# One row tile for the second FFN bias, one product for the shifts, strips of 32 columns, and new step lists

## The chip, the cores and the metric

One core of one Trainium2 chip runs the whole kernel; seven others are idle. The metric is the device time of one execution in microseconds (us), the median of three runs. Five engines work side by side, each through its own list of instructions: TensorE (PE in the profile; its weight loads are shown as PEld), VectorE (DVE), ScalarE (ACT), GpSimd (POOL) and SyncE (SP), which issues the transfers. Semaphores order them.

## What is computed

`x` is 16 images of 16 x 16 positions with 96 channels, so 4096 tokens. Cut to what matters, the reference is:

```python
x = x + leaky_relu(top-2 of 5 experts, mixed(groupnorm(x) @ We + be))     # "conv"
t = tokens(x)                                                             # [16, 256, 96]
n = layernorm(t)
k, q, v = n @ wk, n @ wq, n @ wv                                          # 6 heads of 16
wei = softmax(causal(k @ q.T / 96**0.5))                                  # 256 x 256 a head
t = t + (wei @ v) @ wproj + bproj
n = layernorm(t)
h = gelu(n @ w1[e] + b1[e])                                               # 4 experts, 384 hidden
y = h @ w2[e] + b2[e]                                                     # b2: the second FFN bias
t = t + sum over e of weight[e] * y[e]                                    # top 2 of 4
```

All inputs and outputs are float32.

## The kernel before, in words

The 16 images are worked on in eight units of two images, so 512 tokens (four tiles of 128) a unit. A step is named `kind.index@unit`, and `ORDER` holds one list of steps for each engine, written out by a planner; the order of the work is that of these lists, and semaphores hold each step until its data is there. A step of TensorE carries the PSUM bank it writes after a colon. `warm.6@0:1` are six products that compute nothing used and fill a wait.

The steps that matter here:

- `conv`, `norm1_t`, `qk`, `score`, `prob`, `gate2`: whole products or transposes of up to 128 columns.
- `v` (L872), `proj` (L961) and the products of `ffn2` (L1010): float32 products with the tokens as the stationary side, in strips of `STRIP` = 64 tokens, which write 64 partitions of PSUM each and can run two side by side. A float32 product is two instructions in the trace. `pv` (L946) has always been 32 columns wide, four side by side.
- `ffn1.m` (L988, L989): the first FFN layer of one block of 128 hidden columns, two products of 512 tokens. The rest of its contraction, 32 of the rows, is done for three blocks at once by `rest1.e` (L994): three products of 32 rows each at partitions 0, 32 and 64. It is a step of its own in the list. ScalarE's GELU (L793) of a block waits for it.
- `ffn2.e` (L996 to L1014): the second layer of expert `e`. First the bias, a product of 128 rows (`ones_b` times `b2_parts`, L1003), whose three parts of b2 stand at rows 0, 32 and 64 with zeros between them; GpSimd puts them there (L616 to L622). Then 24 float32 products in strips, which are 48 instructions. VectorE adds the result to the residual (L1266).
- `shift`: VectorE splits the negated row maxima of the scores into three bfloat16 parts (L1182 to L1195), TensorE turns them, one transposition of 18 columns for each of four tiles (L912 to L915), ScalarE copies the [18, 512] result (L758), and SyncE places it in `k_stack` (L513), where the products of `prob` need it.

Of the kernel before, what the change touches and what calls it, by code (L numbers as in the profile page):

```python
# [30 lines left out]
STRIP = 64  # L31
# [35 lines left out]
        prob.0.1@1:5 prob.0.2@1:0 prob.0.3@1:6 prob.0.4@1:4 prob.1.0@1:1 prob.1.1@1:5 proj@0:3 prob.1.2@1:0
        prob.1.3@1:6 conv.3@5:4 prob.1.4@1:2 warm.3@12:1 score.0.0@2:1 score.0.1@2:5 score.0.2@2:0 score.0.3@2:3
        score.0.4@2:6 score.1.0@2:2 score.1.1@2:4 norm2_t@0:1 score.1.2@2:5 pv.0@1:0 score.1.3@2:3 norm1_t@3:6
        score.1.4@2:2 pv.1@1:1 qk.0@3:4 qk.1@3:5 gate2@0:6 ffn1.0@0:0 ffn1.1@0:4 ffn1.2@0:5 rest1.0@0:-1 ffn1.3@0:3  # L70
        ffn1.4@0:2 proj@1:1 ffn1.5@0:0 rest1.1@0:-1 ffn1.6@0:4 ffn1.7@0:5 ffn1.8@0:3 rest1.2@0:-1 shift@2:2 ffn2.0@0:0
# [1225 lines left out]
```

## Time and profile before

| | |
|---|---|
| median of three runs | 316.29 us (316.01 to 317.96) |
| the profiled execution | 316.23 us, of which the span of the core is 314.5 |
| granted TensorE clock over the span | 0.998 |
| TensorE, VectorE, ScalarE, GpSimd busy | 94%, 76%, 70%, 34% of the span |

The span runs from the first to the last instruction of the core. Times inside it are counted from its start. TensorE's instructions are pipelined and their ends are modelled, so the busy time of TensorE counts overlapping instructions once, and the time from one start to the next is the better measure of what a product costs.

### The profile page before, as it was taken

To read this page: it belongs to the slowest core of one execution; us is meant where nothing else is said; L and a number is where in the kernel's file an instruction comes from. 1 tells how busy PE (TensorE), PEld (TensorE's weight loads), DVE (VectorE), ACT (ScalarE), POOL (GpSimd) and SP (SyncE) were. 2 spreads that over 40 slices of the span, in tenths; PEclk is the share of its full clock that TensorE was granted. 3 is DMA by queue.
4 is the path that set the end of the run, shared out by engine and by line. 5 is a ranking of instruction groups with operands and counts; after the bars stand their busy time and mean duration, and the time that the engine had idled before them with its cause. 6 is when DMAs were issued, how large, how long until landed. Compare 5 with 4: busy or idle time off the path is not lost.

```text
span 314.5 us, 9387 instructions
## 1 busy us (share of the span) xinstructions
PE 297.0 (94%) x3459; PEld 214.7 (68%) x3459; DVE 238.7 (76%) x1050; ACT 221.1 (70%) x441; POOL 106.3 (34%) x176
## 2 busy tenths in 40 slices
PE   5889899998999999999999999999999999999995
PEld 2655445665656877778677786777686787877774
DVE  4769989997899898898899788799738845813433
ACT  2879778886678997787766495773986769472660
POOL 4444567549821450065070006720622041100000
PEclk9999999999999999999999999999999999999999
DMA  7930054625637010034133003610380111002000
GB/s 178 185 41 0 1 120 72 113 83 125 101 82 115 4 45 0 4 96 113 36 81 95 4 3 77 128 31 14 87 112 3 29 27 44 0 10 62 2 27 25
DMA packets 28436, 18.70 MB, mean 59 GB/s; under 512 B 16820, under 2 KB 26952, under 8 KB 28392
## 3 DMA queue, kind: packets, MB, share of 16 engines
q1 hardware_dynamic: 28392, 18.12, 27.4%
q8 instruction: 27, 0.44, 0.7%
q14 instruction: 17, 0.14, 0.2%
HBM read 3.12 MB, written 1.57 MB: 15 GB/s over the span
## 4 chain that ended last, share of the span: by engine, by line
PE 65%; SPq 2%; DMA 1%; ACT 1%; DVE 1%; issue 1%; POOL 1%; DVEq 0%; POOLq 0%; ACTq 0%
PE PS L1010 21%; PE PS L988 8%; PE PS L989 7%; PE PS L994 4%; PE PS L946 4%; PE PS L961 3%; PE PS L862 3%; PE PS L904 2%; PE PS L928 2%; PE PS L1003 2%; PE PS L854 2%; SPq L509 2%; PE PS L893 1%; DMA k_stack<-qk_parts 1%; PE PS L932 1%; PE PS L975 1%
## 5 line engine op out<-in xcount | busy, mean ns | idle before, releaser
L793 ACT ACTIVATE hidden<-PS,b_t 128x512 f32<-128x512 f32 x96 | 59.5, 683 | 33.1 <-PE PS L994 32.9
L1010 PE MATMUL PS<-w_f,hidden 128*64 128x96 f32 x1536 | 70.4, 248 | 0.0
L1010 PEld LDWEIGHTS PS<-w_f,hidden 128*64 128x64 f32 x1536 | 64.4, 137 | 7.0 <-issue 7.0
L1266 DVE SCALAR_TENSOR_TENSOR res<-PS,weight,res 128x96 f32<-128x96 f32 x128 | 31.4, 309 | 35.5 <-PE PS L1010 35.2
L988 PE MATMUL PS<-t_a,w_a 128*128 128x512 f32 x96 | 42.0, 437 | 0.0
L989 PE MATMUL PS<-t_b,w_b 128*128 128x512 f32 x96 | 37.9, 395 | 0.0
L1170 DVE CUSTOM_DVE_ANT_0 masked<-PS,causal 128x128 bf16<-128x128 f32 (+1 forms) x120 | 34.9, 352 | 3.6 <-PE PS L893 2.1
L769 ACT ACTIVATE prob_a<-PS 128x512 f32<-128x512 f32 x48 | 25.9, 601 | 10.8 <-PE PS L928 10.7
L654 POOL TENSOR_SCALAR_AFFINE_SELECT prob_a<-prob_a 128x768 f32<-128x768 f32 x16 | 13.8, 865 | 57.0 <-ACT prob_a L769 57.0
L1131 DVE SCALAR_TENSOR_TENSOR PS<-conv_y,weight,PS 128x96 f32<-128x96 f32 x128 | 30.2, 316 | 2.5 <-ACT PS L721 2.4
L575 POOL TENSOR_TENSOR ln_var<-ln_mv,eps_t 128x4 f32<-128x4 f32 x16 | 3.2, 198 | 74.6 <-DVE ln_mv L1063 74.6
L666 ACT ACTIVATE normed<-res,ln_bias,ln_scale 128x96 f32<-128x96 f32 x64 | 24.6, 458 | 2.7 <-POOL ln_bias L585 2.7
L988 PEld LDWEIGHTS PS<-t_a,w_a 128*128 128x128 f32 x96 | 18.1, 188 | 7.0 <-issue 1.6
L814 PE MATMUL PS<-ones_b 128*128 128x512 bf16 x89 | 22.7, 397 | 0.0
L989 PEld LDWEIGHTS PS<-t_b,w_b 128*128 128x128 f32 x96 | 18.1, 189 | 2.2
L648 POOL TENSOR_TENSOR qk_parts<-qk_rest,qk_parts 96x512 bf16<-96x512 f32 x16 | 18.5, 1158 | 2.4
L711 ACT ACTIVATE conv_y<-PS 128x486 f32<-128x486 f32 x32 | 17.1, 566 | 1.9 <-PE PS L803 1.5
L1181 DVE TENSOR_REDUCE row_max<-PS 128x2 f32<-128x512 f32 (+2 forms) x30 | 16.9, 626 | 0.5 <-PE PS L893 0.5
L862 PE MATMUL PS<-t,qk_w 96*96 96x512 f32 x32 | 15.9, 610 | 1.1 <-ACT t L736 1.0
L904 PE MATMUL PS<-q_stack,k_stack 96*128 96x256 bf16 x96 | 16.8, 273 | 0.0
L582 POOL TENSOR_TENSOR ln_scale<-ln_var,power_t 128x4 f32<-128x4 f32 x16 | 16.2, 1012 | 0.0
L769 ACT ACTIVATE prob_b<-PS 128x512 f32<-128x512 f32 (+1 forms) x32 | 14.7, 499 | 2.0 <-PE PS L932 2.0
(157 smaller groups left out, 613.4 us busy)
## 6 DMA issues: line engine op xcount, KB each, us to landing
q_stack<-qk_parts SPq DMA_DIRECT2D x48, 96.0 KB, 3.2
k_stack<-qk_parts SPq DMA_DIRECT2D x48, 96.0 KB, 3.7
t_c<-t_a SPq DMA_DIRECT2D x24, 64.0 KB, 2.0
out_dram<-res SPq DMA_DIRECT2D x8, 192.0 KB, 2.5
X<-in_x_dram SPq DMA_DIRECT2D x4, 192.0 KB, 2.9
X<-in_x_dram SPq DMA_DIRECT2D x2, 384.0 KB, 5.1
...
```

Of the source, the lines that this page charges most:

```text
L666: act.activation(normed[:, which, t, :], rows[:, t, :], ACT.Identity, bias=ln_bias[:, which, t:t + 1], scale=ln_scale[:, which, t:t + 1]). ...
L769: act.activation(dst, PS[:, bank("prob", n, index), 0:dst.shape[1]], ACT.Exp, scale=SCALE).then_inc(act_emptied["prob"], 1)
L793: act.activation(hidden[:, m, 0:T * P], PS[:, bank("ffn1", n, index), 0:T * P], ACT.Gelu, bias=b1_t[:, m:m + 1]).then_inc(act_emptied["ffn ...
L814: pe.matmul(PS[:, bank("warm", n, index), :], ones_b[:, :], ones_b[:, :].unsqueeze(1).to_broadcast([P, 4, P]), start=True, stop=True)
L862: pe.matmul(PS[0:C, bank("qk", n, index), 0:T * P], qk_w[:, tensor, :], t1s[n % 2][:, 0:T * P], start=True, stop=True).then_inc(filled["qk ...
L904: mm = pe.matmul(dst[:, j * TOKENS:(j + 1) * TOKENS], kk[0:STACK, h, t0 + P:t0 + TOKENS], q[0:STACK, h, t0:t0 + TOKENS], start=n >= MASK_FROM,
L988: pe.matmul(dst, w1_a[:, w], t2_as[n % T2][:, 0:T * P], start=True, stop=False)
L989: pe.matmul(dst, w1_b[:, w], t2_bs[n % T2][:, 0:T * P], start=False, stop=False)
L1010: mm = pe.matmul(PS[strip:strip + STRIP, y, t * C:(t + 1) * C], hidden[:, m, t * P + strip:t * P + strip + STRIP], w2_f[:, m, :], start=Fa ...
L1131: ins = dve.scalar_tensor_tensor(mixed[:, t, :], y, weight0[:, t, e:e + 1], mixed[:, t, :], ALU.mult, ALU.add)
L1170: ins = dve.tensor_tensor_reduce(masked[:, place % 2, j * size:(j + 1) * size], ps[:, j * size:(j + 1) * size], causal[:, TOKENS - size:TO ...
L1266: ins = dve.scalar_tensor_tensor(res2[:, t, :], PS[:, y, t * C:(t + 1) * C], weight1[:, t, e:e + 1], res2[:, t, :], ALU.mult, ALU.add).the ...
```

## The change

- `STRIP` goes from 64 to 32, so `v`, `proj` and `ffn2` have twice as many products, each half as wide.
- The three parts of b2 go to rows 96, 97 and 98 of `b2_parts`. GpSimd splits b2 on one partition, and three transfers of SyncE (`w_b2`) place the parts. The bias product has three rows instead of 128. The zero fills of `b2_f` and `b2_parts` on VectorE go, and b2 is loaded once instead of three times.
- `rest1.e` of the experts 1 to 3 goes into `ffn2.(e-1)`, ahead of its bias; `rest1.0` stays a step. The wait for the expert's GELU moves behind the bias.
- The shift parts lie as [part, head, tile], so one transposition of 72 columns turns them, ScalarE copies [72, 128], and the transfer places 72 rows of 128.
- All five lists are new. TensorE's has 429 steps instead of 459, with 68 warm-up products instead of 89 (counted in the lists).

The lists are cut here to some of their lines.

```diff
@@ -28,7 +28,7 @@
-STRIP = 64
+STRIP = 32
@@ -54,129 +54,125 @@
     PE: """
-        xt@0:0 warm.6@0:1 gavg.0@0:1 xt@1:2 xt@2:3 gavg.1@0 xt@3:4 warm.4@1:5 xt@4:5 xt@5:6 gavg.0@1:0 warm.2@2:2
-        xt@6:2 xt@7:1 gavg.1@1 conv.0@0:3 conv.1@0:4 conv.2@0:5 conv.3@0:6 warm.14@3:2 conv.0@1:2 conv.1@1:0 conv.2@1:1
-        conv.3@1:3 warm.9@4:4 conv.0@2:4 conv.1@2:5 conv.2@2:6 conv.3@2:2 warm.16@5:0 norm1_t@0:0 conv.0@3:1 conv.1@3:3
-        gavg.0@2:4 warm.2@6:5 qk.0@0:5 qk.1@0:6 warm.13@7:2 norm1_t@1:2 conv.2@3:1 conv.3@3:0 warm.3@8:3 gavg.1@2
-        warm.10@9:3 qk.0@1:3 qk.1@1:5 score.0.0@0:6 score.0.1@0:1 score.0.2@0:0 score.0.3@0:4 v@0:2 v@1:3 score.0.4@0:6
-        score.1.0@0:5 score.1.1@0:1 norm1_t@2:0 score.1.2@0:4 score.1.3@0:2 score.1.4@0:3 conv.0@4:6 conv.1@4:5
-        conv.2@4:1 conv.3@4:4 qk.0@2:2 warm.2@10:6 shift@0:6 qk.1@2:3 warm.5@11:0 score.0.0@1:0 score.0.1@1:5
...
-        rest1.1@7:-1 ffn2.3@6:2 ffn1.7@7:6 ffn1.8@7:1 ffn2.0@7:0 ffn1.9@7:3 ffn1.10@7:2 ffn1.11@7:4 rest1.2@7:-1
-        rest1.3@7:-1 ffn2.1@7:0 ffn2.2@7:5 ffn2.3@7:6
+        xt@0:0 warm.6@0:1 gavg.0@0:1 xt@1:2 xt@2:3 gavg.1@0 xt@3:4 warm.9@1:5 gavg.0@1:5 xt@4:6 xt@5:0 xt@6:2 xt@7:1
+        gavg.1@1 conv.0@0:3 conv.1@0:4 conv.2@0:6 conv.3@0:0 warm.13@2:2 gavg.0@2:2 conv.0@1:1 conv.1@1:5 conv.2@1:3
+        conv.3@1:4 conv.0@2:6 conv.1@2:0 gavg.1@2 conv.2@2:1 conv.3@2:5 conv.0@3:3 conv.1@3:4 conv.2@3:2 conv.3@3:6
+        norm1_t@0:0 qk.0@0:1 qk.1@0:5 v@0:0 warm.22@3:3 norm1_t@1:3 qk.0@1:4 warm.6@4:2 score.0.0@0:2 qk.1@1:6
+        score.0.1@0:1 score.0.2@0:5 score.0.3@0:0 score.0.4@0:3 score.1.0@0:4 conv.0@4:2 score.1.1@0:1 score.1.2@0:5
+        score.1.3@0:0 score.1.4@0:6 conv.1@4:3 conv.2@4:4 norm1_t@2:1 conv.3@4:5 warm.9@5:0 qk.0@2:0 shift@0:6 qk.1@2:2
+        score.0.0@1:3 score.0.1@1:1 score.0.2@1:4 score.0.3@1:5 score.0.4@1:6 score.1.0@1:3 score.1.1@1:1 warm.3@6:4
...
+        ffn1.2@7:5 ffn1.3@7:4 ffn1.4@7:3 ffn1.5@7:0 rest1.0@7:-1 ffn2.3@6:1 ffn2.0@7:2 ffn1.6@7:6 ffn1.7@7:5 ffn1.8@7:1
+        ffn1.9@7:4 ffn1.10@7:3 ffn1.11@7:0 ffn2.1@7:2 ffn2.2@7:6 ffn2.3@7:5
...
     SCALAR: """
-        norm1@0 conv.3@2 conv.0@3 leaky@1 norm1_t@0 tanh@2 conv.1@3 qk.0@0 qk.1@0 mix@2 norm1@1 w_w1@0 conv.2@3
+        norm1@0 conv.3@2 norm1_t@0 conv.0@3 conv.1@3 conv.2@3 qk.0@0 conv.3@3 leaky@1 qk.1@0 tanh@2 xn@4 mix@2 v@0
...
     GPSIMD: """
-        groot@0 xn@0 groot@1 xn@1 mask@0 w_b2.0@0 w_b2.1@0 xn@2 rstd1@0 xn@3 w_b2.2@0 rstd1@1 qk.0@0 qk.1@0 groot@2
-        rstd1@2 qk.0@1 xn@4 qk.1@1 xn@5 xn@6 prob.0.0@0 prob.0.1@0 prob.1.0@0 prob.1.1@0 qk.0@2 qk.1@2 w_w1@0
+        groot@0 xn@0 groot@1 xn@1 xn@2 xn@3 rstd1@0 groot@2 qk.0@0 mask@0 rstd1@1 qk.1@0 xn@4 rstd1@2 qk.0@1 qk.1@1
+        w_b2.0@0 xn@5 qk.0@2 prob.0.0@0 prob.0.1@0 prob.1.0@0 prob.1.1@0 xn@6 qk.1@2 w_b2.1@0 w_w1@0 w_b2.2@0 rstd2@0
+        rstd1@3 prob.0.0@1 prob.0.1@1 prob.1.0@1 prob.1.1@1 qk.0@3 qk.1@3 rstd2@1 rstd1@4 xn@7 prob.0.0@2 prob.0.1@2
...
     SYNC: """
-        stk.0@0 stk.2@0 stk.4@0 stk.1@0 stk.3@0 stk.5@0 stk.0@1 stk.2@1 stk.4@1 stk.1@1 stk.3@1 stk.5@1 shift@0
-        w_w1.0@0 stk.0@2 shift@1 stk.2@2 stk.4@2 stk.1@2 stk.3@2 stk.5@2 w_w1.1@0 t2@0 stk.0@3 stk.2@3 stk.4@3 stk.1@3
+        stk.0@0 stk.2@0 stk.4@0 stk.1@0 stk.3@0 stk.5@0 stk.0@1 stk.2@1 stk.4@1 stk.1@1 stk.3@1 stk.5@1 shift@0 stk.0@2
+        shift@1 stk.2@2 stk.4@2 stk.1@2 stk.3@2 stk.5@2 w_w1.0@0 w_w1.1@0 t2@0 w_b2@0 stk.0@3 stk.2@3 stk.4@3 stk.1@3
...
@@ -322,9 +318,9 @@
         row_max = sb("row_max", [P, TILES, HEADS])
-        shift_parts = sb("shift_parts", [P, TILES, SHIFT, HEADS], BF16)
-        shift_rest = sb("shift_rest", [P, TILES, HEADS])
-        shift_t = sb("shift_t", [SHIFT * HEADS, PT], BF16)
+        shift_parts = sb("shift_parts", [P, SHIFT, HEADS, TILES], BF16)
+        shift_rest = sb("shift_rest", [P, HEADS, TILES])
+        shift_t = sb("shift_t", [SHIFT * HEADS * TILES, P], BF16)
         prob_a = sb("prob_a", [P, 2, HEADS, TOKENS])
@@ -354,9 +350,10 @@
         wv_f = hidden[0:C, 4, 2 * C:3 * C].rearrange("c (h d) -> c h d", d=D)
-        b2_f = hidden[0:65, 5, 0:E1 * C]
-        b2_rest = hidden[0:65, 6:8, 0:E1 * C]
-        b2_lead = hidden[0:65, 8, 0:E1 * C].bitcast(BF16).rearrange("p (a n) -> p a n", a=2)
+        b2_f = hidden[0:1, 5, 0:E1 * C]
+        b2_rest = hidden[0:1, 6:8, 0:E1 * C]
+        b2_lead = hidden[0:1, 8, 0:E1 * C].bitcast(BF16).rearrange("p (a n) -> p a n", a=2)
+        b2_last = hidden[0:1, 6, 0:E1 * C // 2].bitcast(BF16)
@@ -385,6 +382,7 @@
         b2_split = sem("b2_split")
+        b2_placed = sem("b2_placed")
@@ -415,9 +413,9 @@
-        CONV_PADS, PADS, LATE_PADS = 5, 6, 2
+        CONV_PADS, PADS, LATE_PADS = 4, 5, 2
         W1_COPIES, T2_COPIES = 3 + CHUNKS, 2 + CHUNKS
-        FFN_LOADS = 12
+        FFN_LOADS = 10
         STACK_DMAS = 2 * len(K_PARTS)
@@ -461,7 +459,7 @@
                          (w2_f[:, :, :], w2.rearrange("e (k p) c -> p (e k) c", p=P))]
-            ffn_loads += [(b2_f[r:r + 1, :], b2.rearrange("(a e) c -> a (e c)", a=1)) for r in (0, 32, 64)]
+            ffn_loads.append((b2_f[:, :], b2.rearrange("(a e) c -> a (e c)", a=1)))
             wproj_heads = wproj.rearrange("(h d) c -> d h c", d=D)
@@ -510,7 +508,8 @@
                     wait_act(sp, "shift", n)
-                    sp.dma_start(k_stacks[n % 2][STACK:STACK + SHIFT, :, 0:T * P], shift_t[:, 0:T * P]).then_inc(shift_placed, 16)
+                    sp.dma_start(k_stacks[n % 2][STACK:STACK + SHIFT, :, :].rearrange("p h (a t) -> p (h a) t", t=P),
+                                 shift_t[:, :]).then_inc(shift_placed, 16)
                 elif kind == "w_w1":
@@ -522,6 +521,11 @@
                             sp.dma_start(w1_c[j * REST:(j + 1) * REST, :, :].bitcast(F32), rest[:, :, j, :]).then_inc(w1_placed, 16)
+                elif kind == "w_b2":
+                    sp.wait_ge(b2_step, 4)
+                    sp.wait_ge(b2_split, 1)
+                    for i, part in enumerate((b2_lead[:, 0, :], b2_lead[:, 1, :], b2_last[:, :])):
+                        sp.dma_start(b2_parts[C + i:C + i + 1, :], part).then_inc(b2_placed, 16)
                 elif kind == "t2":
@@ -614,12 +618,7 @@
                         pool.wait_ge(b2_step, 4)
-                        pool.tensor_copy(b2_parts[0:1, :], b2_lead[0:1, 0, :]).then_inc(b2_split, 1)
-                        pool.wait_ge(b2_split, 1)
-                        pool.tensor_copy(b2_parts[32:33, :], b2_lead[32:33, 1, :]).then_inc(b2_split, 1)
-                        pool.wait_ge(b2_split, 2)
-                        pool.tensor_copy(b2_parts[64:65, :], b2_rest[64:65, 1, :]).then_inc(b2_split, 1)
-                        pool.wait_ge(b2_split, 3)
+                        pool.tensor_copy(b2_last[:, :], b2_rest[:, 1, :]).then_inc(b2_split, 1)
                 elif kind == "mask":
@@ -755,7 +754,7 @@
                         act.wait_ge(shift_placed, 16 * n)
-                    act.activation(shift_t[:, 0:T * P], PS[0:SHIFT * HEADS, bank("shift", n), 0:T * P // 2].bitcast(BF16), ACT.Copy
+                    act.activation(shift_t[:, :], PS[0:SHIFT * HEADS * TILES, bank("shift", n), 0:P // 2].bitcast(BF16), ACT.Copy
                                    ).then_inc(act_emptied["shift"], 1)
@@ -788,7 +787,7 @@
                         act.wait_ge(wv_split, 1)
-                        act.wait_ge(b2_split, 3)
+                        act.wait_ge(b2_placed, 16 * 3)
                     wait_filled(act, "ffn1", n, index)
@@ -801,6 +800,13 @@
                 return pe.matmul(dst, a_lo, b_hi[0:a_lo.shape[0], :], start=False, stop=True)
+
+            def rest_rows(n, e):
+                T = size_of(n)[1]
+                for j in range(CHUNKS):
+                    rows = slice(j * REST, (j + 1) * REST)
+                    pe.matmul(PS[:, bank("ffn1", n, (e * CHUNKS + j,)), 0:T * P], w1_c[rows, e, :],
+                              t2_cs[n % T2][rows, 0:T * P], start=False, stop=True).then_inc(filled["ffn1"], 1)
```

## Rows read from the trace of the kernel before

**Rows 1.** The page, part 1: busy time, share of the span, instructions of each engine.
```profile
PE 297.0 (94%) x3459; PEld 214.7 (68%) x3459; DVE 238.7 (76%) x1050; ACT 221.1 (70%) x441; POOL 106.3 (34%) x176
```

**Rows 2.** Five stretches: busy time of each engine, clock, DMA share, GB/s.
```profile
core 0: us, PE busy (x) PEld busy (x) DVE busy (x) ACT busy (x) POOL busy (x), PEclk, DMA share, GB/s
0.00:92.20 92.20, 79.92 (x584) 50.51 (x584) 75.97 (x279) 68.47 (x156) 50.65 (x88) 1.00 0.45 91
92.20:150.00 57.80, 57.43 (x727) 43.08 (x727) 52.80 (x249) 48.14 (x97) 21.00 (x33) 1.00 0.26 58
150.00:200.00 50.00, 49.94 (x620) 37.22 (x619) 43.72 (x207) 33.99 (x70) 14.69 (x22) 1.00 0.21 53
200.00:256.00 56.00, 54.87 (x746) 41.17 (x745) 42.05 (x213) 39.39 (x70) 14.44 (x24) 1.00 0.29 53
256.00:311.00 55.00, 54.87 (x790) 42.71 (x788) 23.27 (x101) 31.12 (x52) 5.54 (x11) 1.00 0.08 21
```

**Rows 3.** Groups of TensorE: line, shapes, count, busy us, mean ns, idle before.
```profile
L1010 PE MATMUL PS<-w_f,hidden 128*64 128x96 f32 x1536 | 70.4, 248 | 0.0
...
L814 PE MATMUL PS<-ones_b 128*128 128x512 bf16 x89 | 22.7, 397 | 0.0
```

**Rows 4.** TensorE in order of time: start, us, instruction, count; unit 6.
```profile
294.51 0.40 PE L988 MATMUL PS<-t_a,w_a 128*128 128x512 f32 x1
294.75 0.39 PE L989 MATMUL PS<-t_b,w_b 128*128 128x512 f32 x1
295.07 0.50 PE L994 MATMUL PS<-t_c,w_c 32*128 32x512 f32 x3
295.50 0.34 PE L1003 MATMUL PS<-b_parts,ones_b 128*128 128x384 bf16 x1
295.77 2.20 PE L1010 MATMUL PS<-w_f,hidden 128*64 128x96 f32 x48
297.90 0.50 PE L988 MATMUL PS<-t_a,w_a 128*128 128x512 f32 x1
298.24 0.40 PE L989 MATMUL PS<-t_b,w_b 128*128 128x512 f32 x1
```

**Rows 5.** TensorE in order of time, rest products and P V of unit 7.
```profile
262.26 0.49 PE L994 MATMUL PS<-t_c,w_c 32*128 32x512 f32 x3
...
263.14 0.40 PE L946 MATMUL PS<-prob_b,v_aug 128*32 128x128 f32 x8
263.36 0.61 PE L946 MATMUL PS<-prob_a,v_aug 128*32 128x256 f32 x8
263.79 0.40 PE L946 MATMUL PS<-prob_b,v_aug 128*32 128x128 f32 x8
```

**Rows 6.** TensorE in order of time, around a shift and around two short products.
```profile
247.31 0.39 PE L913 MATMUL PS<-ident_b,shift_parts 128*18 128x128 bf16 x4
247.63 0.34 PE L1003 MATMUL PS<-b_parts,ones_b 128*128 128x384 bf16 x1
...
260.20 0.28 PE L932 MATMUL PS<-k_stack,q_stack 99*128 99x128 bf16 x2
260.32 0.60 PE L854 MATMUL PS<-ident,normed 128*96 128x128 f32 x4
```

**Rows 7.** TensorE in order of time, ahead of unit 0's first transpose.
```profile
30.32 3.63 PE L814 MATMUL PS<-ones_b 128*128 128x512 bf16 x16
34.73 0.64 PE L854 MATMUL PS<-ident,normed 128*96 128x128 f32 x4 [0.78 <-ACT normed L666]
```

**Rows 8.** Groups of ScalarE: the largest of four of table loads; the shift's copy.
```profile
L793 ACT ACT_TABLE_LOAD x9 | 11.5, 1283 | 3.2 <-PE PS L994 3.1
...
L758 ACT ACTIVATE shift_t<-PS 18x512 bf16<-18x512 bf16 x8 | 4.7, 584 | 2.7 <-PE PS L913 2.7
```

**Rows 9.** The page, part 3, TensorE's instructions; and a copy's time to landing.
```profile
q8 instruction: 27, 0.44, 0.7%
...
t_c<-t_a SPq DMA_DIRECT2D x24, 64.0 KB, 2.0
```

More of the change, by code:

```diff
@@ L67 @@
[L67 to L71, printed above, removed]
@@ L158 @@
[L158 to L162 removed]
+        gstat@0 gmean@0 w_conv@0 gvar@0 gstat@1 gstat@2 gstat@3 gmean@1 gstat@4 gstat@5 gvar@1 gstat@6 gates.0@0
@@ new lines @@
+        score.1.3@1 score.1.4@1 shift@1 mix.4@3 qk.1@2 gates.1@4 att.0@0 att.1@0 proj@0 xadd@3 stats1@3 score.0.0@2
+        score.0.1@2 score.0.2@2 score.0.3@2 score.0.4@2 score.1.0@2 score.1.1@2 score.1.2@2 score.1.3@2 score.1.4@2
+        mix.1@4 norm2_t@0 qk.0@3 qk.1@3 att.0@1 att.1@1 gates.0@5 shift@2 gate2@0 mix.2@4 proj@1 weights@0 mix.3@4
+        gates.1@5 mix.4@4 ffn2.0@0 ffn2.1@0 xadd@4 norm2_t@1 stats1@4 mix.1@5 mix.2@5 mix.3@5 gate2@1 score.0.0@3
+        ffn2.2@0 score.0.1@3 mix.4@5 score.0.2@3 score.0.3@3 score.0.4@3 score.1.0@3 score.1.1@3 score.1.2@3
@@ new lines @@
+        score.1.3@3 score.1.4@3 shift@3 att.0@2 att.1@2 gates.0@6 ffn2.3@0 weights@1 ffn2.0@1 gates.1@6 proj@2 xadd@5
+        stats1@5 qk.0@4 qk.1@4 mix.1@6 mix.2@6 mix.3@6 norm2_t@2 ffn2.1@1 mix.4@6 gate2@2 weights@2 att.0@3 att.1@3
+        gates.0@7 ffn2.2@1 gates.1@7 proj@3 xadd@6 stats1@6 qk.0@5 mix.1@7 qk.1@5 score.0.0@4 score.0.1@4 ffn2.3@1
+        ffn2.0@2 score.0.2@4 score.0.3@4 score.0.4@4 score.1.0@4 mix.2@7 norm2_t@3 score.1.1@4 score.1.2@4 mix.3@7
+        ffn2.1@2 score.1.3@4 score.1.4@4 shift@4 score.0.0@5 score.0.1@5 score.0.2@5 ffn2.2@2 score.0.3@5 score.0.4@5
@@ new lines @@
+        ffn2.3@2 score.1.0@5 score.1.1@5 score.1.2@5 score.1.3@5 score.1.4@5 shift@5 gate2@3 weights@3 ffn2.0@3 qk.0@6
+        qk.1@6 mix.4@7 ffn2.1@3 att.0@4 att.1@4 ffn2.2@3 proj@4 xadd@7 stats1@7 ffn2.3@3 score.0.0@6 score.0.1@6
+        score.0.2@6 score.0.3@6 score.0.4@6 norm2_t@4 score.1.0@6 score.1.1@6 score.1.2@6 att.0@5 att.1@5 score.1.3@6
+        score.1.4@6 shift@6 gate2@4 proj@5 weights@4 qk.0@7 ffn2.0@4 qk.1@7 norm2_t@5 ffn2.1@4 ffn2.2@4 gate2@5
+        score.0.0@7 score.0.1@7 score.0.2@7 score.0.3@7 score.0.4@7 score.1.0@7 score.1.1@7 score.1.2@7 score.1.3@7
@@ L180 @@
+        stk.2@5 stk.4@5 stk.1@5 stk.3@5 t2@3 stk.5@5 shift@4 shift@5 stk.0@6 store@1 stk.2@6 stk.4@6 store@2 stk.1@6
+        stk.3@6 stk.5@6 t2@4 shift@6 stk.0@7 stk.2@7 stk.4@7 store@3 stk.1@7 stk.3@7 stk.5@7 t2@5 shift@7 t2@6 store@4
+        store@5 t2@7 store@6 store@7
         """}
@@ L911, in _ @@
                     pe.wait_ge(shift_ready, n + 1)
-                    for t in range(T):
-                        mm = pe.transpose(PS[0:SHIFT * HEADS, bank("shift", n), t * P // 2:(t + 1) * P // 2].bitcast(BF16),
-                                          shift_parts[:, t, :, :].rearrange("p a h -> p (a h)"), ident_b[:, :])
-                    mm.then_inc(filled["shift"], 1)
+                    pe.transpose(PS[0:SHIFT * HEADS * TILES, bank("shift", n), 0:P // 2].bitcast(BF16),
+                                 shift_parts[:, :, :, :].rearrange("p a h t -> p (a h t)"), ident_b[:, :]).then_inc(filled["shift"], 1)
                 elif kind == "prob":
@@ L990, in _ @@
                 elif kind == "rest1":
-                    e = index[0]
-                    for j in range(CHUNKS):
-                        rows = slice(j * REST, (j + 1) * REST)
-                        pe.matmul(PS[:, bank("ffn1", n, (e * CHUNKS + j,)), 0:T * P], w1_c[rows, e, :],
-                                  t2_cs[n % T2][rows, 0:T * P], start=False, stop=True).then_inc(filled["ffn1"], 1)
+                    rest_rows(n, 0)
                 elif kind == "ffn2":
```

197 lines of the change are left out of this document (89 added, 108 removed).

## The prediction

> **What bounds the kernel now.** I read the busy line of the page first, then the busy time of each engine in five stretches, then the groups of TensorE instructions, and last the order of time of single TensorE instructions, where the price of each step can be seen. TensorE is busy 94% of the span [rows 1]. The stretches say where that matters [rows 2]: up to 92.2 us, where the first FFN product starts, TensorE is busy 79.9 of 92.2 us, and 89 warm-up products [rows 3] are counted in that, so it waits there. From 92.2 to 311 us it is busy 217.1 of 218.8 us, at the full granted clock (1.00, 2.4 GHz) in every stretch. So after 92 us time saved on TensorE is time saved in the kernel, as long as VectorE follows: it is busy 52.8 of 57.8 us up to 150, 43.7 of 50 up to 200, and 23.3 of 55 at the end. Before 92 us TensorE's work is not what ends last.
>
> **How TensorE spends a step.** Products come in four layouts of the array: whole, 64 columns, 32 columns, and 32 rows (the rest products). [rows 4] shows one FFN block after another. Two whole products of 512 columns stand 0.24 us apart (294.51, 294.75). From the last of them to the rest products it is 0.32 (294.75, 295.07): 0.09 more, for emptying the array when the layout changes. Behind a change back, the first product takes 0.34 to the next start (297.90, 298.24) instead of 0.24: its weights could not be loaded ahead, 0.10. The three rest products run together, yet hold TensorE 0.43 (295.07, 295.50). The bias product holds it 0.27 (295.50, 295.77), of which about 0.10 is the change to the 64-column strips, so 0.17 is the product. Then 48 strip products take 2.13 (295.77, 297.90).
>
> **Strips of 32.** P V already runs in 32 columns [rows 5]: eight products of 256 columns take 0.43 us (263.36, 263.79), eight of 128 columns 0.22 (263.14, 263.36). Each such eight is two rounds over four strips side by side, so a round costs 0.215 and 0.11: in proportion to the columns, with no fixed part to be seen. For 96 columns a round is 0.215 x 96/256 = 0.081. The 64-column form of now has 24 rounds of two (48 products): 24 x 0.081 = 1.94 of its 2.13. The 32-column form has 96 products in 24 rounds of four, so the same 1.94. What goes is half of the first weight load. The longest entry shown, 0.10 for 128 columns, makes 0.05 for 64 and 0.025 for 32: 0.025 in each of 48 groups (32 in the FFN, 8 of V, 8 of the projection), 1.2 us. The other end: no row shows products closer together for long than 0.22/8 = 27 ns, and 32-column strips want 81/4 = 20 ns. At 27 ns, 7 ns too many over 3840 products (twice 1536 [rows 3], 256 and 128) are +27, less some ends of groups that overlap, say +22. I take the proportional end, since two row lengths lie on one line through zero.
>
> The Trainium skill, in TensorE: Matmul & The Clock Gate, section "Wait — 56ns, not 53.3ns?", says that starts of matmuls never come closer than about 25 ns. By it an FFN group would take 96 x 25 = 2.4 us and the kernel about 321. The trace is against it across tiles: three rest products are over 0.49 us after the first has begun (262.26) [rows 5], and one whole product of as many columns lasts 0.40 to 0.51 [rows 4], so they start almost at once. For 96 products in a row no run here shows it. It is rival (a) below.
>
> **Bias in the fourth row tile.** Three rows at partition 96 make the bias a 32-row product, like the rest products at 0, 32 and 64, and the code now issues it right behind them. For 24 of 32 experts it runs beside them: 24 x 0.17 = 4.1 us gone. For the last expert of a unit it stands alone and keeps its time. Had the fourth tile to wait for the other three, nothing of the 4.1 would come.
>
> **Shift.** Four transposes of 18 columns are a 32-column layout, one of 72 is not. Now it is four products in 0.32 us with the change behind them (247.31, 247.63) [rows 6]; a single one of this size costs 0.06 (260.20, two in 0.12). Three fewer in eight units: 24 x 0.06 = 1.4.
>
> **Changes of layout.** I counted them through both TensorE lists: 173 now, 127 after. The bias needs none of its own, the shift none, the rest products lead straight into the strips instead of back to whole products, and V, the projection, P V and the FFN strips can follow each other. Each costs 0.09 for emptying and, with what follows, 0.05 to 0.10 of weights; at the low end 46 x 0.14 = 6.4.
>
> Sum on TensorE: 1.2 + 4.1 + 1.4 + 6.4 = 13.1. Seven of the changes and two of the shifts lie ahead of the first FFN product, about 1.3 us where TensorE waits anyway. Left: **-11.8**.
>
> **The lists ahead of 92 us.** Nearly the same steps stand there, with 68 warm-up products for 89. At 0.22 us each (16 in 3.63, and still 0.78 idle behind them) [rows 7] that is 4.6 us less filler. The order also lets unit 0 pass: its transpose is copied before the next unit's convolution rows, and GpSimd does the second and third residual of x before it splits the bias. VectorE is busy 76 of 92 us there, so not all can be had: between 0 and -4.6 I take half, **-2.3**.
>
> **VectorE behind 92 us.** Between 92.2 and 200 us it works 96.5 of 107.8. If TensorE needs some 6 us less there, VectorE would be at 95%, and steps that depend on each other do not run that tight; between 0 and +6 I take **+2**.
>
> **What I price at nothing.** Two fills leave VectorE's start, ahead of its first data. The shift copy on ScalarE shrinks from 0.59 us [rows 8], not on the path. ScalarE loads its tables about 22 times, by my count of GELU and exponential steps in its list, for 18 now (four groups, the largest has 9), 4 x 1.28 us more [rows 8]; it is busy 57 to 70% after 150 us, and there this is covered; without cover it would be 5 us. The bias now needs three small transfers, which SyncE issues behind the first t2 copies, and the first GELU waits for them. Queued behind them are the stacks of unit 3, first used at its scores, which stand behind three experts of unit 0 in TensorE's list; the GELU waits for the rest products anyway. If the transfers came 2 us [rows 9] after t2, most of that is under the first three blocks. The shift's transfer is cut in 72 runs for 18; scores of the next unit stand between it and its use. The rest products wait inside the step of the expert before, so GELU of an expert starts later in the list; three blocks of GELU need about 2 us, and the strips beside which they run take as long.
>
> **The sum.** The profiled execution took 316.2 us (span 314.5 and 1.7 around it), the median is 316.3, so the two agree. 316.2 - 11.8 - 2.3 + 2 = **304**.
>
> **Rivals.** (a) Strips limited by the product, not the columns: 27 ns a product, +22, so 326. From 24 ns on (12 us / 3840 = 3 ns over 20) the whole gain is gone. For it: nothing shows 96 products closer. Against it: the proportion in [rows 5]. 8%. (b) Instructions arrive too late: 27 blocks served 3459 products with as many weight loads [rows 1, 9], some 260 a block, used up in about 5.7 us of strips now and in 2.8 then; copies of 64 KB land after 2.0 us. If each of the 30 blocks that the strips then take came 0.5 us late, 319. 5%. (c) VectorE takes back 6 instead of 2, or the fourth tile does not overlap (+4), or both: 308 to 312, 20%. (d) The lists bring all 4.6 and VectorE none: 299 to 300, 7%. (e) The early part becomes longer by 5 with (c): 315, 5%. My forecast, 300 to 308, has 55%.
>
> About 1% (3 us) is what a measurement of this kernel can tell from no change. Faster by over 1% is the forecast, (c) and (d): 0.82; within 1%, (e) and part of (b): 0.07; slower, (a) and the rest of (b): 0.11. The range runs from 299 to 312, leaving out (a), (b), (e).
>
> **What will show it.** 96 strip products of an FFN group in about 2.1 us; if 2.5, (a). Bias starting within 0.02 us of the three rest products, and 0.43 from them to the strips; else (c). First FFN product at 88 to 91 us. Waits of TensorE for VectorE between 90 and 200 us of some 2 us. Long gaps before weight loads with no releaser inside the strips would mean (b).

## The result and the profile after

The changed kernel takes **312.61 us** (median of 4 runs, 312.28 to 313.13), the kernel before 316.15 on the same chip: ratio 0.987, interval 0.983 to 0.9915. A second measurement gave 313.08 for 316.58, ratio 0.988 (0.984 to 0.992). So it became 3.5 us faster. 304 had been forecast (304.1 by the terms of the sum), 299 to 312; the profiled execution took 313.13 us, so 9.0 us of it have to be explained.

The page after, busy time, granted clock of TensorE in 40 slices, and fetched instructions (before: [rows 1, 9]):

```profile
PE 287.9 (92%) x5334; PEld 209.7 (67%) x5334; DVE 237.1 (76%) x1048; ACT 223.9 (72%) x445; POOL 104.7 (34%) x174
...
PEclk9999669999999999999899999999999999999999
...
q8 instruction: 42, 0.69, 1.0%
```

In the changed kernel L992 and L993 are the first FFN layer, L808 its rest products, L1004 the bias, L1012 the strips of the second layer, L860 the transposes behind a layer norm, L868 the query and key products, L878 V, L950 P V, L965 the projection, L977 and L979 the gate, L800 to L802 the convolution, L918 the shift and L820 the warm-up products, here called fillers. In some runs these lines stand a line or two further up or down.

Busy time in five stretches, as in [rows 2]; the first one ends where the first FFN product starts:

```profile
core 0: us, PE busy (x) PEld busy (x) DVE busy (x) ACT busy (x) POOL busy (x), PEclk, DMA share, GB/s
0.00:93.86 93.86, 78.28 (x663) 49.37 (x663) 74.87 (x279) 69.79 (x159) 51.03 (x87) 0.95 0.47 89
93.86:150.00 56.14, 54.81 (x1044) 40.97 (x1040) 51.56 (x244) 48.56 (x97) 19.31 (x32) 0.97 0.24 54
150.00:200.00 50.00, 48.72 (x1058) 36.13 (x1054) 41.24 (x209) 30.28 (x61) 11.74 (x19) 1.00 0.19 47
200.00:256.00 56.00, 54.40 (x1244) 41.26 (x1240) 45.42 (x217) 41.03 (x74) 16.28 (x26) 1.00 0.24 63
256.00:307.73 51.73, 51.67 (x1357) 41.93 (x1345) 23.06 (x98) 34.28 (x57) 6.36 (x12) 1.00 0.11 28
```

Three things differ from before. The first FFN product starts at 93.86 us, not 92.2. Behind it TensorE is busy 209.6 of 213.9 us: it now waits 4.3 us there, for 1.7 before. And the granted clock is no longer 1.00 everywhere.

TensorE in order of time, one FFN block of unit 6 (start, us; before: [rows 4]):

```profile
286.55 0.50 PE L808 MATMUL PS<-t_c,w_c 32*128 32x512 f32 x3
286.56 0.33 PE L1004 MATMUL PS<-b_parts,ones_b 3*128 3x384 bf16 x1
286.98 2.19 PE L1012 MATMUL PS<-w_f,hidden 128*32 128x96 f32 x96
289.09 0.50 PE L992 MATMUL PS<-t_a,w_a 128*128 128x512 f32 x1
289.43 0.39 PE L993 MATMUL PS<-t_b,w_b 128*128 128x512 f32 x1
```

The bias starts 0.01 us after the rest products and costs nothing: from the rest products to the strips it is 0.43, as it was without a bias. The 96 strip products take 2.11 us here, the 48 of before took 2.13; the medians over all FFN groups are 2.118 and 2.132.

The new lists have no filler ahead of unit 0's transpose, where [rows 7] had 16. TensorE there, and its clock two us at a time (us of the stretch, busy, granted clock):

```profile
30.39 0.38 PE L802 MATMUL PS<-conv_hi,xn_lo 96*128 96x486 f32 x1
34.87 1.06 PE L860 MATMUL PS<-ident,normed 128*96 128x128 f32 x4 [4.11 <-ACT normed L665]
36.66 3.70 PE L868 MATMUL PS<-t,qk_w 96*96 96x512 f32 x4 [0.73 <-issue]
```

```profile
core 0: us, PE busy (x), PEclk, DMA share, GB/s
34.00:36.00 2.00, 1.06 (x4) 0.50 0.00 0
...
42.00:44.00 2.00, 2.00 (x6) 0.51 0.75 155
44.00:46.00 2.00, 2.00 (x11) 1.00 1.17 137
```

After 4.11 us without a product the granted clock is 0.50 (1.2 GHz), and it is back at 1.00 (2.4 GHz) only from 44 us. A second such place lies behind 92 us:

```profile
145.03 0.25 PE L979 MATMUL PS<-gate_hi,t_b 96*128 96x4 f32 x1
145.86 0.61 PE L860 MATMUL PS<-ident,normed 128*96 128x128 f32 x4 [0.58 <-ACT normed L665]
146.41 1.08 PE L950 MATMUL PS<-prob_a,v_aug 128*32 128x256 f32 x8
```

```profile
146.00:147.00 1.00, 1.00 (x12) 0.69 0.59 169
147.00:148.00 1.00, 1.00 (x20) 0.50 0.59 153
148.00:149.00 1.00, 1.00 (x20) 0.50 0.34 78
149.00:150.00 1.00, 1.00 (x20) 0.61 0.52 127
```

Ahead of it stand eight gate products of 4 and 8 columns, with a wait of 0.18 in front of them, and a wait of 0.58 behind them. Eight P V products of 256 columns then last 1.08 us instead of the 0.61 of [rows 5]; (0.31 + 0.50 + 0.50 + 0.39) x 1 us is 1.7 us of clock that is missing here.

### The profile page after: what moved, and what is told of

Read it like the earlier page. It is cut to its first block, busy times and chain, and to the rows that moved or that the text cites. A ratio compares the mean times of both kernels' runs of the same rounds, so it can differ in the third digit from the quotient of the medians.

```text
span 311.4 us, 13113 instructions
## 1 busy us (share of the span) xinstructions
PE 287.9 (92%) x5334; PEld 209.7 (67%) x5334; DVE 237.1 (76%) x1048; ACT 223.9 (72%) x445; POOL 104.7 (34%) x174
## 4 chain that ended last, share of the span: by engine, by line
PE 47%; DVE 20%; issue 8%; ACT 6%; POOL 5%; SPq 4%; DMA 2%; DVEq 0%; POOLq 0%; ACTq 0%
PE PS L1012 17%; PE PS L992 6%; PE PS L993 5%; PE PS L950 4%; SPq L507 4%; PE PS L965 2%; PE PS L808 2%; DMA k_stack<-qk_parts 2%; ACT normed L665 2%; DVE res L1266 2%; PE PS L868 2%; POOL ln_scale L586 2%; DVE masked L1170 2%; DVE PS L1131 2%; DVE row_max L1181 2%
## 5 line engine op out<-in xcount | busy, mean ns | idle before, releaser
L1012 PE MATMUL PS<-w_f,hidden 128*32 128x96 f32 x3072 | 70.0, 247 | 0.0
L1012 PEld LDWEIGHTS PS<-w_f,hidden 128*32 128x32 f32 x3072 | 63.1, 110 | 7.5 <-issue 7.3
L992 PE MATMUL PS<-t_a,w_a 128*128 128x512 f32 x96 | 42.9, 447 | 1.7 <-DVE res L1266 0.7
L993 PE MATMUL PS<-t_b,w_b 128*128 128x512 f32 x96 | 37.9, 395 | 0.0
L768 ACT ACTIVATE prob_a<-PS 128x512 f32<-128x512 f32 x48 | 26.6, 604 | 5.3 <-PE PS L932 5.0
L992 PEld LDWEIGHTS PS<-t_a,w_a 128*128 128x128 f32 x96 | 18.1, 188 | 10.3 <-issue 2.6
L993 PEld LDWEIGHTS PS<-t_b,w_b 128*128 128x128 f32 x96 | 18.1, 189 | 3.4 <-issue 1.0
L868 PE MATMUL PS<-t,qk_w 96*96 96x512 f32 x32 | 18.1, 672 | 2.1 <-ACT t L735 1.0
L820 PE MATMUL PS<-ones_b 128*128 128x512 bf16 x68 | 17.9, 415 | 0.0
L950 PE MATMUL PS<-prob_a,v_aug 128*32 128x256 f32 x192 | 16.4, 413 | 0.6 <-issue 0.5
L808 PE MATMUL PS<-t_c,w_c 32*128 32x512 f32 x96 | 16.0, 491 | 0.4 <-DVE t_b L1149 0.3
```

Source lines behind the costliest of these rows:

```text
L768: act.activation(dst, PS[:, bank("prob", n, index), 0:dst.shape[1]], ACT.Exp, scale=SCALE).then_inc(act_emptied["prob"], 1)
L868: pe.matmul(PS[0:C, bank("qk", n, index), 0:T * P], qk_w[:, tensor, :], t1s[n % 2][:, 0:T * P], start=True, stop=True).then_inc(filled["qk ...
L950: mm = pe.matmul(PS[HS * j:HS * (j + 1), bank("pv", n, index), first_t:(r % 2 + 1) * TOKENS], v_augs[n % 2][:, 2 * image + half, h, :], pr ...
L992: pe.matmul(dst, w1_a[:, w], t2_as[n % T2][:, 0:T * P], start=True, stop=False)
L993: pe.matmul(dst, w1_b[:, w], t2_bs[n % T2][:, 0:T * P], start=False, stop=False)
L1012: mm = pe.matmul(PS[strip:strip + STRIP, y, t * C:(t + 1) * C], hidden[:, m, t * P + strip:t * P + strip + STRIP], w2_f[:, m, :], start=Fa ...
```

## The experiments

Each run had the kernel before beside it on the same chip. The table gives the difference of the two medians, and, of the profiled execution, which can be any of the runs, the start of the first FFN product and the time from there to the last product (before 92.2 and 218.7).

| run | what | us | to before | first FFN | from there |
|---|---|---|---|---|---|
| changed | | 312.61 | -3.5 | 93.9 | 213.9 |
| a_again | the same once more | 313.08 | -3.5 | 93.4 | 212.7 |
| lists_only | new lists, old products | 319.90 | +3.4 | 93.9 | 220.3 |
| oldlists_none | old lists, new products but the bias | 315.09 | -1.4 | 92.1 | 219.1 |
| a_bias128 | bias of 128 rows | 318.64 | +2.4 | 94.5 | 218.2 |
| a_shift4 | four transposes a shift | 314.21 | -2.2 | 94.9 | 214.4 |
| a_strip64 | strips of 64 columns | 312.02 | -4.2 | 94.4 | 212.6 |
| a_fill16 | 16 fillers, unit 0 | 311.11 | -5.1 | 93.6 | 211.5 |
| a_fill_early | 16 fillers, earlier | 311.59 | -4.9 | 93.6 | 212.6 |
| a_fill_both | fillers at two places | 312.10 | -4.1 | 93.5 | 211.9 |
| a_u1 | unit 1's norm first | 313.94 | -2.6 | 94.5 | 212.7 |
| a_dveearly | a_fill16, lighter VectorE early | 311.51 | -4.9 | 96.4 | 211.8 |
| a_dvelate | a_fill16, lighter VectorE late | 307.58 | -8.9 | 93.1 | 208.8 |
| b_dvelate | before, lighter VectorE late | 315.51 | -1.0 | 91.8 | 218.4 |
| a_oldearly | early part in the old order | 314.36 | -2.2 | 95.2 | 213.4 |

The intervals of the ratios are 0.5 to 1% wide (1.5 to 3 us), so differences of 1 to 2 us between two rows are not certain.

### Products and lists apart

**lists_only**: the lists of the changed kernel, with `STRIP = 64`, the bias of 128 rows behind the rest products, and four transposes a shift.

> The new lists with the old products: strips of 64 columns, a second FFN bias of 128 rows, four transposes a shift; only the order of the work is that of the changed kernel. Theory 1 (the new lists cost time of their own, in the early part and in waits of TensorE behind it, and hide a part of what the products save): 319.5 to 322, 3 to 6 us longer than the kernel before. Theory 2 (the lists are neutral and the products save less than I summed): 315 to 317.

Measured 319.9 us, ratio 1.011 (1.0075 to 1.014): theory 1. The two stretches, ahead of the first FFN product and behind it:

```profile
0.00:93.91 93.91, 78.98 (x573) 0.95 0.44 89
93.91:314.21 220.30, 218.15 (x2867) 1.00 0.19 46
```

Against [rows 2], 1.7 us are lost ahead of the first FFN product and 1.6 behind it. The loss ahead belongs to the lists and not to the products: the first FFN product starts at 93.9 us with new lists and old products, at 92.1 with old lists and new products (oldlists_none below). From there the new products bring 3.4 + 3.5 = 6.9 us. (With the old products the lists are not those that a planner would have made for them; the 3.4 us are what this order costs them.)

**a_bias128**, **a_shift4** and **a_strip64** each take one product back in the changed kernel (the code of the first and the last; the shift is that of the kernel before, with its copy and its transfer):

```diff
-                    pe.matmul(..., ones_b[C:C + 3, :], b2_parts[C:C + 3, ...]...to_broadcast([3, T, C]), ...
+                    pe.matmul(..., ones_b[:, :], b2_parts[:, ...]...to_broadcast([P, T, C]), ...
-STRIP = 32
+STRIP = 64
```

> The changed kernel, its lists included, with the second FFN bias as a product of 128 rows again (parts of b2 at rows 96 to 98, zeros elsewhere), so that it can't run beside the three rest products. Theory 1 (after 92 us TensorE's work sets the time): 24 products of 0.27 us and their change of layout come back, 6.5 to 8 us, so 319 to 320.6. Theory 2 (VectorE sets the pace after 92 us, and the hidden bias was worth little): less than 4 us more, 313 to 316.

> The changed kernel with four transposes of 18 columns a shift again (and the copy and transfer that go with them), all else as changed. Theory 1, my terms (24 x 0.06 us of products, and 11 more changes of layout by count through the list, at 0.14): 3.0 us longer, 315.6. Theory 2 (the changes of layout around a shift are covered by waits that are there anyway, and the products alone count): 0.5 to 1.7 us longer, 313.1 to 314.3.

> The changed kernel with strips of 64 columns for V, the projection and the second FFN layer, all else as changed. Theory 1, my term (first weights of 32 columns 0.025 us sooner in 48 groups, and V, projection, P V and FFN strips that follow each other without a change of layout): 1 to 2 us longer, 313.6 to 314.6. Theory 2, by the groups of the changed kernel (95 starts 20.4 ns apart make 1.94, as 47 of 42 ns did): the form of the strips is worth 0.5 us at most, so 312.6 to 313.1.

The bias is worth 2.4 + 3.5 = 5.9 us, just under the 6.5 to 8 of theory 1. Its trace shows the old block again, 0.43 and then 0.27:

```profile
296.00 0.50 PE L808 MATMUL PS<-t_c,w_c 32*128 32x512 f32 x3
296.43 0.34 PE L1004 MATMUL PS<-b_parts,ones_b 128*128 128x384 bf16 x1
296.70 2.19 PE L1012 MATMUL PS<-w_f,hidden 128*32 128x96 f32 x96
```

The shift is worth 1.3 us, in the range of theory 2, though its interval overlaps that of the changed kernel. But theory 2's reason, that the changes of layout around the shift cost nothing, is not what the traces show. Here is the same shift, between first-layer and rest products, with one product and, in a_shift4, with four:

```profile
224.91 0.39 PE L993 MATMUL PS<-t_b,w_b 128*128 128x512 f32 x1
225.14 0.22 PE L918 MATMUL PS<-ident_b,shift_parts 128*72 128x128 bf16 x1
225.29 0.50 PE L808 MATMUL PS<-t_c,w_c 32*128 32x512 f32 x3
```

```profile
226.42 0.40 PE L994 MATMUL PS<-t_b,w_b 128*128 128x512 f32 x1
226.75 0.39 PE L918 MATMUL PS<-ident_b,shift_parts 128*18 128x128 bf16 x4
227.07 0.51 PE L807 MATMUL PS<-t_c,w_c 32*128 32x512 f32 x3
```

The way into the four is 0.33 us for 0.23, so that change costs 0.10, and the four hold TensorE 0.32 for 0.15. TensorE's busy time behind the first FFN product is 2.1 us longer in a_shift4 (211.7 for 209.6). The strips are worth nothing that can be measured (64 columns came out 0.6 us faster): below even theory 2. The sum, 5.9 + 1.3 - 0.6 = 6.6, agrees with the 6.9 of lists_only within the intervals.

**oldlists_none**: the old lists with 32-column strips, one transposition a shift, and the bias of three rows as a product of its own, since the old lists have the rest products elsewhere. (By a reading of the old lists, the bias can't go beside the rest products there for most experts, because the banks of the next blocks are reused ahead of `ffn2`; no run shows it.)

> The old lists with the new products as far as they go with them: strips of 32 columns, one transposition a shift, a bias of three rows at partitions 96 to 98, but as a step of its own and not beside the rest products, whose step stays where it was. Theory 1 (what TensorE saves is the kernel's, as long as the lists stay): the shift's 1.4 to 2 us and the strips' 0.5 to 1, so 313.3 to 314.3. Theory 2 (with these lists too, other engines take back what TensorE saves): 315.5 to 316.5.

Measured 315.09, 1.4 us better than before, ratio 0.996 (0.994 to 0.998): between the theories. The size is that of the shift above; the run does not tell the shift from the strips. Its profiled execution, 316.65 us, was the longest of its 12, so its row of the table is not a typical one.

### The clock

```diff
-        conv.3@3:6 norm1_t@0:0 qk.0@0:1
+        conv.3@3:6 warm.16@7:0 norm1_t@0:0 qk.0@0:1          # a_fill16
-        gate2@2:0 norm1_t@5:1
+        gate2@2:0 warm.3@8:1 norm1_t@5:1                     # a_fill_both, with the first
```

> The changed kernel with 16 more warm-up products in TensorE's list, ahead of unit 0's first transpose, where TensorE stood still for 4.1 us and its granted clock was then at the lower of its two levels up to about 46 us. Theory 1, the clock: the query and key products of unit 0 (3.70 us, for 1.93 in the kernel before) get their 1.8 us back, the granted clock is 1.00 from 32 to 48 us, the first FFN product starts at about 92 instead of 93.9 us, and the time is about 310.8. Theory 2, the order of the new lists makes the early part as long as it is, and other engines set it: the clock is 1.00 as well, but the first FFN product stays at 93.5 to 94 and the time at 312 to 313.

> The changed kernel with the 16 warm-up products ahead of unit 0's first transpose and three more ahead of unit 5's, where TensorE waited 0.58 us at 145.3 us and worked at the lower clock from 146.3 to 149.4. Theory 1 (what TensorE loses to the clock after 92 us is lost for the kernel): another 1.5 us, so about 309.3, and the granted clock of the whole span is 1.00. Theory 2 (after 92 us another engine sets the pace as well): the time is that of the run with the first filler alone, within 0.5 us.

> The changed kernel with 16 warm-up products ahead of unit 3's convolution, so that no bank has to be waited for, and TensorE goes on to unit 0's transpose with no wait over 1.5 us. Theory 1 (the clock alone): clock 1.00 in the early part, unit 0's transpose at 34.9, its query and key products in 1.9 us, the first FFN product at 92 to 92.5, the time 310. Theory 2 (the order of the lists on the other engines): the first FFN product at 93.3 to 94, the time within 0.5 us of the run with 16 fillers right ahead of the transpose, 311.1.

a_fill16 took 311.11 us, 1.6 less than the changed kernel against the same kernel before. Its early part:

```profile
33.21 3.63 PE L820 MATMUL PS<-ones_b 128*128 128x512 bf16 x16 [1.48 <-ACT conv_y L710]
36.68 0.60 PE L860 MATMUL PS<-ident,normed 128*96 128x128 f32 x4
38.01 1.93 PE L868 MATMUL PS<-t,qk_w 96*96 96x512 f32 x4 [0.73 <-issue]
```

```profile
0.00:93.64 93.64, 79.00 (x679) 1.00 0.47 89
93.64:305.16 211.52, 208.31 (x4675) 1.00 0.20 49
```

The query and key products take 1.93 us again instead of 3.70, but the filler waited for a bank and held the transpose back by 1.8. The first FFN product hardly moved (theory 2 for the early part); in the profiles what was won lies behind it, 211.5 for 213.9, where the clock is now 1.00 throughout. a_fill_early, whose filler waits for no bank and whose clock is 1.00 up to the first FFN product, has it at 93.6 too. So the low clock of the early part is not what makes that part long.

What the second fall of the clock costs is less sure. In a_fill16 nothing was added near 145 us, and the same eight gate products, with waits of 0.15 and 0.57 us around them, were not followed by a fall:

```profile
145.65 0.61 PE L860 MATMUL PS<-ident,normed 128*96 128x128 f32 x4 [0.57 <-ACT normed L665]
146.19 0.64 PE L950 MATMUL PS<-prob_a,v_aug 128*32 128x256 f32 x8
```

```profile
146.00:147.00 1.00, 1.00 (x23) 1.00 0.44 128
147.00:148.00 1.00, 1.00 (x32) 1.00 0.62 154
```

The fall is there in the profiled executions of a_again, a_shift4 and a_fill_early, and absent from those of a_strip64 and a_u1, behind the same products and waits. So it comes and goes by the execution, and no run shows what decides it. From the first FFN product on, a_again and a_fill_early take 212.7 and 212.6 us with the fall, a_fill16, a_fill_both and a_dveearly 211.5 to 211.9 without, and a_u1 212.7 without: about 1 us or less, and the rest of the 2.4 between 213.9 and 211.5 is a difference of executions. So the profile of a_fill16 has no fall that a filler at 145 us could remove, and a_fill_both is no sharp test of one: it took 312.10 us, against the 309.3 of theory 1, not measurably apart from a_fill16, and its time behind the first FFN product is 211.9.

The kernel before is not free of falls either. In 25 of its 78 executions beside these runs the clock over the span was 0.992 to 0.995, and they took 317.6 to 318.9 us; the other 53 had 0.998 or more and took 315.2 to 317.1. The profile of before is one of the latter. All ten executions of the changed kernel had 0.976 to 0.989.

### VectorE

Sums over the experts take 24 of 96 columns, which makes VectorE's instructions shorter and leaves their number; the other 72 columns of these sums are left out. In a_dvelate and b_dvelate it is the sum of the FFN (shown) and, for units 4 to 7, that of the convolution; in a_dveearly it is that of the convolution for units 0 to 3:

```diff
-                            res2[:, t, :], PS[:, y, t * C:(t + 1) * C], weight1[:, t, e:e + 1], res2[:, t, :],
+                            res2[:, t, 0:24], PS[:, y, t * C:t * C + 24], weight1[:, t, e:e + 1], res2[:, t, 0:24],
```

> The changed kernel with 16 warm-up products ahead of unit 0's transpose, and VectorE's work behind 92 us made lighter: the sum over the experts in the FFN and, for units 4 to 7, in the convolution takes 24 of 96 columns (the rest of the output is left out). Theory 1 (VectorE's pace is what TensorE waits for behind 92 us): TensorE's idle time there falls from 3.2 to 1.5 us or less and its busy time, which holds short waits, by another 1 to 2 us, so 308 to 309.2 for 311.1. Theory 2 (the waits come from the order of the lists and from ScalarE): 310.5 or more.

> The control: the kernel before with VectorE's work behind 92 us made lighter in the same way (24 of 96 columns in both sums over experts; the rest of the output is left out). TensorE waits only 1.6 us there. Theory 1: at most 1.5 us shorter, 314.7 to 316. Theory 2: no change, 316 to 316.5.

> The changed kernel with 16 warm-up products ahead of unit 0's transpose, and VectorE's work ahead of 92 us made lighter: the sum over the experts of the convolution takes 24 of 96 columns for units 0 to 3 (the rest of that sum is left out). Theory 1 (VectorE's work sets the early part of the new lists): the first FFN product starts 2 us or more earlier, at 91.5 or less, the time 309 or less. Theory 2 (the early part is a chain over GpSimd, ScalarE and transfers in which VectorE waits as well): the first FFN product at 92.5 to 93.6, the time 310 to 311.

The changed kernel with the filler gains 3.8 us from a lighter VectorE behind 92 us (307.58, ratio 0.972, 0.967 to 0.976), a little more than theory 1; the kernel before gains 1.0 (ratio 0.9975, 0.9945 to 1.0005). The stretches behind the first FFN product of a_dvelate and of b_dvelate:

```profile
93.14:301.92 208.78, 207.06 (x4675) 1.00 0.20 50
```

```profile
91.83:310.27 218.44, 216.79 (x2878) 1.00 0.21 46
```

With VectorE out of the way TensorE needs 208.8 us, of which it is busy 207.1; in the kernel before the same relief changes 218.7 to 218.4. The waits of TensorE behind 93.8 us in the changed kernel (us, times, longest) name VectorE in eight of ten lines; the four longest are:

```profile
PE PS L992 <- DVE res L1266: 0.7, 1, 0.7
PE PS L992 <- DVE row_max L1170: 0.6, 1, 0.6
PE PS L860 <- ACT normed L665: 0.6, 1, 0.6
PE PS L965 <- DVE XT L1219: 0.4, 1, 0.4
```

A lighter VectorE ahead of 92 us brought nothing that can be measured (311.51, for 311.11 of a_fill16), which is nearer to theory 2. Its profile can't be used for the early part: that execution was the longest of its six, had its first FFN product at 96.4 us, in neither range, and a granted clock of 0.96 up to there.

### The order ahead of the first FFN product

The transpose behind unit 1's layer norm comes 4.7 us later in the changed kernel, 3.8 with the filler of a_fill16 (before, then changed):

```profile
42.84 0.64 PE L854 MATMUL PS<-ident,normed 128*96 128x128 f32 x4 [0.37 <-ACT normed L666]
```

```profile
47.58 0.60 PE L860 MATMUL PS<-ident,normed 128*96 128x128 f32 x4
```

**a_u1** puts unit 1's layer norm ahead of unit 0's query residual again; **a_oldearly** puts all steps that the new lists have ahead of the first FFN product into the old order.

```diff
 GPSIMD, a_u1
-        xn@3 rstd1@0 groot@2 qk.0@0 mask@0 rstd1@1
+        xn@3 mask@0 rstd1@0 groot@2 rstd1@1 qk.0@0
```

> The changed kernel with 16 warm-up products ahead of the last unit's convolution of the early part (unit 3), 14 instead of 22 ahead of unit 1's transpose, and unit 1's layer norm ahead of unit 0's query residual again on GpSimd, VectorE and ScalarE, as in the kernel before. Theory 1 (the new lists let unit 0 pass and make unit 1's norm late, at 46.6 to 47.6 instead of 43 us, and that is what the early part pays): the transpose of unit 1 at 43 to 44.5 us, the first FFN product at 91 to 92, the time 308 to 309.5. Theory 2 (VectorE's and GpSimd's whole work in the early part sets it, in whatever order): the first FFN product at 93 or later and 310.5 to 312.

> The changed kernel with the steps that its lists have ahead of the first FFN product put into the order (and the banks, and the warm-up products) of the lists before, on all five engines; from the first FFN product on the lists are the new ones, and all products are the new ones. Theory 1 (the new order of the early part costs, by waits and by the clock): the first FFN product starts at 91 to 92.5 us, the granted clock is 1.00 up to there, and the time is 309.5 to 311. Theory 2 (the early part has to be as long as it is for what the new lists want done ahead of the FFN): the first FFN product at 93.5 or later, and 312 or more.

> The changed kernel once more, on the same chip and against the same runs of the kernel before, as the measure for the other run: 312 to 313 by both theories.

Both came out slower than the changed kernel (313.94 and 314.36), and the first FFN product starts at 94.5 and 95.2 us, so by the numbers theory 1 failed in both. But each run had a disturbance of its own. In a_u1 the transpose of unit 1 came at 45.3 us, not at 43 to 44.5: the clock was at the lower level ahead of it (the 14 fillers there took 4.93 us, the 22 of a_fill16 as long), so it tells little of the order. In a_oldearly the early part runs as before up to unit 3's query and key products, which start at 88.96 us (89.59 before, 88.57 in the changed kernel), and then comes a wait at the seam between the old and the new part of the lists, behind which the clock falls to 0.50 for 96 to 98 us:

```profile
88.96 1.96 PE L870 MATMUL PS<-t,qk_w 96*96 96x512 f32 x4
93.61 0.87 PE L880 MATMUL PS<-wv_w,t 96*32 96x96 f32 x32 [2.69 <-DVE row_max L1183]
```

So the new order reaches that product 1.0 us sooner, but with less done. P V of unit 1 (2.0 us) and V of units 2 and 3 (1.4 us) come behind it and ahead of the FFN; the old order had P V of unit 1 and V of unit 2 done before it, had V of unit 3 later, and put only the gate of unit 0 (1.2 us) in that place. Whether another order would have kept both is open.

## Why the prediction was wrong

The forecast was a sum, 316.2 - 11.8 - 2.3 + 2. Term by term, in us of the profiled executions:

| step | forecast | found | from |
|---|---|---|---|
| TensorE's work behind the first FFN product | -11.8 | -10.0 | busy 217.1 [rows 2], 207.1 in a_dvelate |
| VectorE's waits there | +2 | +2.7 | 211.5 in a_fill16, 208.8 in a_dvelate |
| clock, and other differences of the two executions | none | +2.4 | 213.9 and 211.5 (1.2 in a_again) |
| the part ahead of the first FFN product | -2.3 | +1.7 | 92.2 and 93.9 (1.2 in a_again) |

The misses add up to 8.9 of the 9.0 us.

**The lists ahead of 92 us** are the largest miss, 4.0 us. The prediction counted 21 warm-up products fewer as 4.6 us less filler and took half of it as a gain. A filler costs nothing where TensorE would wait anyway: TensorE is busy 78.3 of 93.9 us there, for 79.9 of 92.2, so in the end the filler was replaced by waits and by products at the lower clock, not by an earlier start of the FFN. "The order also lets unit 0 pass" was an argument without a price: unit 0's transpose starts at 34.87 us, for 34.73 before [rows 7], and unit 1's at 47.6 (46.6 in a_fill16) for 42.8. In the trace the work that the order put off, P V of unit 1 and V of two units, stands in front of the FFN instead. That the lists and not the products cost this time is shown (lists_only, oldlists_none); which of the moved steps makes the 1.2 to 1.7 us was not settled. It is not the clock (a_fill_early), and a_dveearly gives no sign that it is VectorE's load.

**The clock** was no term at all. The profile of before had 1.00 in every row, and the prediction took that as given. At 34 to 37 us fillers that the prediction counted as waste had a part in that: in all six profiles of the new lists without them the clock falls there, for 7 to 10 us, and in four of the six with 16 put back it does not (a_fill16, a_fill_early, a_fill_both and a_dvelate; in a_u1 and a_dveearly it does). They do not settle it: in a_fill_both and a_dvelate it falls at 47 us instead. The fall of 3 us at 146 us comes in some executions only. How much of the 2.4 of the table is the clock stays open; the profiles with and without the second fall put that fall at about 1 us or less.

**The price of a change of layout**, 0.14 a piece, was too high: the rows give about 0.10. For the bias the forecast was 0.17 for the product and 0.14 for its change, 7.4 us for 24 experts. The rows show 0.43 + 0.27 = 0.70 before and 0.43 after, so 0.27 each; 29 of the 32 biases, not 24, run beside rest products (for five units the last expert's stands behind those of the next unit), which makes 7.8 us of TensorE's time, and 5.9 us of the kernel's. Around the shift it was 11 changes by the count put down for a_shift4, or 1.5 us, beside 1.4 of products; TensorE got about 2 of these 3 us, and the kernel's time shows 1.3. An estimate for the 1.8 us that the first row of the table lacks: at 0.10 instead of 0.14 the 39 changes behind the first FFN product are 1.6 less, the strips 0.5 less, and five more hidden biases 0.9 more, together 1.2.

**Strips of 32**: 1.2 us forecast from a sooner first weight load. A group went from 2.132 to 2.118 us, 48 x 0.014 = 0.7 us, and the time does not show it. What the prediction had right is that 32-column products run in proportion to their columns: 96 in 2.11 us are one every 22 ns. Rival (a), 27 ns, falls. The Trainium skill (TensorE: Matmul & The Clock Gate, "Wait — 56ns, not 53.3ns?") has about 25 ns as the least distance of two starts; across strips these rows do not agree, and the measurement decides.

**Bias in the fourth row tile**: right in kind. It starts 0.01 us after the three rest products, and the strips follow 0.43 us after these, as forecast.

**VectorE behind 92 us**: right in kind, and near in size. +2 had been put down; a_dvelate against a_fill16 shows 2.7 in the profiles, and 3.8 less 1.0 of the control, 2.8, in the times. Rival (c), 308 to 312 at 20%, was the nearest to what happened, but needed the early part and the clock on top of it. A longer early part was in rival (e), with (c), at 5% and outside the range; that joint case, with 1.7 us instead of 5, is what came.

**Rival (b)**, late instructions: 42 blocks were fetched for 27 [rows 9], and no wait behind the first FFN product had to be put down to them. It falls. **What I priced at nothing** (ScalarE's tables, the small transfers of b2, the shift's 72 runs) shows in no wait of TensorE over 0.3 us behind the first FFN product; the table loads came to 22, as counted.

Of the kernels that compute the whole output, the changed one with 16 fillers at unit 0 has the lowest median: a_fill16, 311.11 us, ratio 0.984 (0.980 to 0.989). Its lead over the changed kernel is 1.6 us by the medians, with intervals that overlap, so it is not certain.
